# Low-rank products by sample on four column positions, with A copied for each sample

## The chip, the core and the metric
One NeuronCore of a Trainium2 chip runs the whole program. The metric is the device time of one execution in microseconds. The times are medians over runs; the profile is one further execution.

## The reference
```
x = x + einsum('bct,bcd->bdt', x, W0[cond])           # x 64x32x512, W0 16x32x32: mixes the 32 rows of a sample
base  = einsum('bsi,oi->bso', x, W)                   # W 512x512
low   = einsum('bsi,bir->bsr', x, lora_A[label])      # lora_A 5x512x32, label 0, 1 or 2 for each of 64 samples
delta = einsum('bsr,or->bso', low, lora_B_w) * 0.5    # lora_B_w 512x32
x = x + base + delta
```
Everything is float32. The kernel treats the label as any of 0 to 4.

## The kernel before
Four samples of 32 rows make a tile of 128 rows; there are 16 tiles, two to a pair, four to a quad. The two linear steps are taken in the other order: first u = x·(M) + delta for each tile, then the mix of the 32 rows of each sample with W0[cond] + identity. M is Wᵀ + identity, to which half the product of A0 (the A of label 0) and B is added in lora_half (L635). It is held as a rounded float32r part m_hi and the rest m_lo, x likewise as xt_hi and xt_lo, and main_tile (L579) makes 12 matmuls per tile from them: hi·hi, hi·lo and lo·hi for each of four chunks c of the 512 inputs.

For the other labels low_pair (L568) multiplies the differences A1..A4 minus A0, side by side in 128 columns (ad_hi, ad_lo), with the 256 rows of a pair, in 12 float32r matmuls. VectorE multiplies the result with keep, a mask by label and sample (keep_low, L450), ScalarE and VectorE split it into kept_hi and kept_lo, and fold_pair (L590) spreads the surviving block on TensorE. ScalarE copies it to low_stack (stack_low, L364), and delta_tile (L595) adds one matmul of low_stack with b_stack, which holds the rounded part and the rest of B/2 in turn.

Each engine has a queue of its own, written by hand, with semaphores between them. TensorE: six warm-up matmuls (L655), transposes of Bw, A, x rows and W with the ident matrix, the two halves of lora_half, then main_tile of the first pair in halves by columns. For each quad from the second on: low_pair, mix_quad (L604: 16 float32 products of 32x32 weights and 512 columns, on 4 row and 4 column positions), the main tiles with fold_pair between them, the delta tiles, low_pair for the second pair and its tiles. The last quad is mixed in three steps (mix_two, then mix_one twice) so that its output can be stored piece by piece. VectorE transposes x in blocks of 32 (transpose_x, L426), makes the lo parts (split_x, L438) and copies every second u out of PSUM (copy_u, L445); ScalarE makes the hi parts (L326), the other copies of u (L331) and the copies of y (L336). GpSimd makes the identity, the row numbers, a_diff (L290), ad_lo and 16 gathers of W0 rows (L264), and mix_of (L300) for each quad. SyncE issues B, the first x_rows, four parts of W, the second x_rows, A1..A4, then x pair by pair into two buffers, each load after the transposes that free its buffer, and the stores between them.

## Time and profile before

| | us |
|---|---|
| median of 3 runs | 84.39 (84.02 to 85.27) |
| profiled execution, its own time | 85.05 |
| its span, first to last instruction | 82.9 |
| TensorE matmuls busy | 76.3 (92%) |
| VectorE busy | 42.9 (52%) |
| ScalarE busy | 33.8 (41%) |
| GpSimd busy | 25.8 (31%) |
| mean granted TensorE clock | 0.986 |

PE is TensorE's matmul side and PEld its weight loads, which overlap; DVE is VectorE, ACT ScalarE, POOL GpSimd, SP SyncE; a q behind a name is that engine's sequencer. Times are us from the start of the span, L571 is line 571 of the kernel. A matmul's duration includes its way through the array, so the distance from one start to the next is what it costs in a row of matmuls. A group "x4" in a timeline is four instructions merged, with the time from the first start to the last end. The idle time stands in brackets with what ended it.

### The profile page before, as it was taken

Reading aid. Unit: us, or ns where it says so; the run is one execution under the profiler, and the core shown is the slowest. Engines: PE = TensorE matmul, PEld = TensorE weight load, DVE = VectorE, ACT = ScalarE, POOL = GpSimd, SP = SyncE. Lnnn points to the kernel's source line nnn. Section 1 sums busy time; section 2 is a strip of 40 time slices with the busy share of each in tenths; the row PEclk is TensorE's granted clock in tenths of the full one; section 3 lists DMA queues with packets and bytes.
Section 4 is the critical chain, followed back from the end, with each engine's and each line's share of the span. In section 5 each row is a group of like instructions: output and inputs, shape, how many; then the busy total and the mean of one; then the engine's idle time right before and its main releaser. Section 6 shows DMA issues by size and latency. Waiting matters only on the chain.

```text
span 82.9 us, 1563 instructions
## 1 busy us (share of the span) xinstructions
PE 76.3 (92%) x596; PEld 63.5 (77%) x596; DVE 42.9 (52%) x79; ACT 33.8 (41%) x70; POOL 25.8 (31%) x42
## 2 busy tenths in 40 slices
PE   4979999999999999999999999999999999999700
PEld 4489899999888588898885888988858887899300
DVE  3285666979932594059725950597269305202220
ACT  0625573624442286225422872254229622343320
POOL 4422786787878778750000200000003000000000
PEclk9999999999999999999999999999999999999995
DMA  0899999083280005797260049980000049705555
GB/s 9 274 270 362 172 202 159 17 209 76 70 199 16 13 11 133 207 249 223 73 180 0 0 124 219 205 214 6 0 4 0 0 95 211 201 8 111 142 127 126
DMA packets 13658, 10.18 MB, mean 123 GB/s; under 512 B 1748, under 2 KB 11348, under 8 KB 13652
## 3 DMA queue, kind: packets, MB, share of 16 engines
q1 hardware_dynamic: 12704, 9.64, 48.1%
q0 software_dynamic: 512, 0.26, 1.7%
q10 hardware_dynamic: 436, 0.20, 1.2%
q8 instruction: 4, 0.07, 0.3%
q14 instruction: 2, 0.02, 0.0%
HBM read 5.90 MB, written 4.19 MB: 122 GB/s over the span
## 4 chain that ended last, share of the span: by engine, by line
PE 83%; DMA 7%; SPq 4%; DVE 1%; issue 1%; DVEq 0%
PE p_u L586 16%; PE p_u L587 15%; PE p_u L588 15%; DMA x_rows<-in_x 7%; PE p_y L602 5%; PE p_low L572 5%; PE p_low L576 5%; PE p_low L571 5%; PE p_u L597 4%; SPq L209 3%; PE p_y L586 2%; PE p_y L587 2%; PE p_y L588 2%; PE p_fold L593 1%; PE p_fold L592 1%; PE p_fold L648 1%
## 5 line engine op out<-in xcount | busy, mean ns | idle before, releaser
L586 PE MATMUL p_u<-m_hi,xt_hi 128*128 128x512 f32 (+1 forms) x64 | 23.4, 365 | 0.0
L587 PE MATMUL p_u<-m_lo,xt_hi 128*128 128x512 f32 (+1 forms) x64 | 22.9, 358 | 0.0
L588 PE MATMUL p_u<-m_hi,xt_lo 128*128 128x512 f32 (+1 forms) x64 | 22.8, 356 | 0.0
L266 POOL DMA_INDIRECT w_sel<-in_L_cond_weights,w_row x16 | 16.2, 1011 | 4.6 <-issue 4.6
L428 DVE STREAM_TRANSPOSE xt<-x_sb 128x512 f32<-128x512 f32 x14 | 15.5, 1115 | 0.7 <-DMA x_sb<-in_x 0.7
L586 PEld LDWEIGHTS p_u<-m_hi,xt_hi 128*128 128x128 f32 x64 | 12.1, 189 | 4.3 <-issue 2.9
L448 DVE COPY u_sb<-p_u 128x512 f32<-128x512 f32 (+1 forms) x7 | 4.6, 654 | 18.0 <-PE p_u L597 18.0
L588 PEld LDWEIGHTS p_u<-m_hi,xt_lo 128*128 128x128 f32 x64 | 12.1, 189 | 1.9
L587 PEld LDWEIGHTS p_u<-m_lo,xt_hi 128*128 128x128 f32 x64 | 12.1, 189 | 1.3
L329 ACT ACTIVATE xt_hi<-xt 128x512 fp32r<-128x512 f32 x14 | 8.8, 630 | 4.8 <-DVE xt L428 4.7
L305 POOL TENSOR_TENSOR mix<-w_sel,fold_id 128x128 f32<-128x128 f32 x4 | 2.2, 550 | 25.4 <-PE p_y L602 25.3
L442 DVE TENSOR_TENSOR xt_lo<-xt,xt_hi 128x512 fp32r<-128x512 f32 x14 | 9.5, 683 | 0.8
L334 ACT ACTIVATE u_sb<-p_u 128x512 f32<-128x512 f32 x7 | 4.2, 599 | 10.8 <-PE p_u L597 10.8
L572 PE MATMUL p_low<-xt_lo,ad_hi 128*128 128x256 f32 x32 | 8.0, 283 | 0.0
L571 PE MATMUL p_low<-xt_hi,ad_hi 128*128 128x256 f32 x32 | 8.0, 282 | 0.0
L362 ACT ACTIVATE kept_hi<-kept 128x256 fp32r<-128x256 f32 x8 | 3.4, 419 | 10.7 <-DVE kept L454 10.7
L339 ACT ACTIVATE y_sb<-p_y 128x512 f32 (+1 forms) x12 | 6.8, 597 | 1.1 <-PE p_y L602 1.1
L572 PEld LDWEIGHTS p_low<-xt_lo,ad_hi 128*128 128x128 f32 x32 | 6.1, 191 | 0.2
L571 PEld LDWEIGHTS p_low<-xt_hi,ad_hi 128*128 128x128 f32 x32 | 6.1, 190 | 0.2
L454 DVE TENSOR_TENSOR kept<-p_low,keep 128x256 f32<-128x256 f32 x8 | 3.4, 424 | 5.0 <-PE p_low L576 4.9
L366 ACT ACTIVATE low_stack<-p_fold 128x256 fp32r<-128x256 f32 x8 | 3.0, 380 | 6.3 <-PE p_fold L593 6.3
L576 PE MATMUL p_low<-xt_hi,ad_lo 128*128 128x256 f32 x32 | 5.1, 282 | 0.0
(94 smaller groups left out, 95.7 us busy)
## 6 DMA issues: line engine op xcount, KB each, us to landing
x_sb<-in_x SPq DMA_DIRECT2D x28, 128.0 KB, 3.0
out<-y_sb SPq DMA_DIRECT2D x12, 256.0 KB, 4.0
w_sb<-in_L_cond_W SPq DMA_DIRECT2D x4, 256.0 KB, 4.3
x_rows<-in_x SPq DMA_DIRECT2D x2, 256.0 KB, 4.3
out<-y_two SPq DMA_DIRECT2D x4, 128.0 KB, 2.3
out<-y_one SPq DMA_DIRECT2D x6, 64.0 KB, 1.9
a_sb<-in_L_cond_lora_A SPq DMA_DIRECT2D x1, 256.0 KB, 6.6
w_sel<-in_L_cond_weights,w_row POOLq DMA_INDIRECT x16, 2.4
```

The lines of the kernel that those rows point to most:

```text
L266: nc.gpsimd.indirect_dma_start(out=w0_sel[:, t, :], out_offset=None, in_=W0_rows, in_offset=bass.IndirectOffsetOnAxis(ap=w0_row[:, t:t + 1 ...
L329: nc.scalar.activation(xt_hi[:, slot, :, P * u:P * (u + 1)], xt[:, u], COPY).then_inc(s_xhi, 1)
L339: nc.scalar.activation(y_sb[:, bass.ds(k, 1), i], p_y[i][:].unsqueeze(1), COPY).then_inc(s_y_copied, 1)
L428: nc.vector.transpose(xt[:, u].rearrange("p c (b s) -> p c b s", s=S), x_sb[:, slot, u].rearrange("p b (i c) -> p c b i", c=C)).then_inc(s ...
L442: nc.vector.tensor_tensor(xt_lo[:, slot, :, cols], xt[:, u], xt_hi[:, slot, :, cols].bitcast(F32), ALU.subtract).then_inc(s_xlo, 1)
L448: nc.vector.tensor_copy(u_sb[:, j, cols], bank[:, cols]).then_inc(s_u_odd, 1)
L571: mm(p_low[:, 0:ROWS], ad_hi[:, c], xt_hi[:, slot, c], start=(c == 0), stop=False)
L572: mm(p_low[:, 0:ROWS], ad_hi[:, c], xt_lo[:, slot, c], start=False, stop=False)
L576: last = mm(p_low[:, 0:ROWS], ad_lo[:, c], xt_hi[:, slot, c], start=False, stop=(c == C - 1))
L586: mm(to, xt_hi[:, slot, c, rows], m_hi[:, c, cols], start=(c == 0 and half != 1), stop=False)
L587: mm(to, xt_hi[:, slot, c, rows], m_lo[:, c, cols], start=False, stop=False)
L588: mm(to, xt_lo[:, slot, c, rows], m_hi[:, c, cols], start=False, stop=False)
```

## The change
- The low products are made sample by sample in float32. For a tile, a chunk c and a sample b, one matmul has the 32 columns of x of that sample as weights (128x32) and the 32 columns of that sample's A as moving data, and writes the 32 rows of the sample in p_low. The four samples of a tile lie on four column positions. 256 such calls take the place of 96 matmuls (low_group).
- Each sample's A comes from a_sel. For each quad GpSimd copies the first 8 samples' A (128x128 each) and ScalarE the other 8, with the offset read from the label into a register (select_a).
- VectorE copies the result four times side by side (copy_low), TensorE transposes it by tile (spread_low), ScalarE rounds all of it into low_stack, and VectorE puts the rest into the lower two of the four blocks (rest_of_low). b_stack holds B/2 rounded, rest, rounded, rest. The mask, the fold and both their splits go.
- Label 0 is no longer part of M: lora_half, the transposes of A and a_diff go. A is loaded whole, 320 KB in place of 64 + 256. B is loaded on ScalarE's queue, in rows of 512 bytes, no longer at the head of SyncE's; it is widened by ScalarE and transposed on TensorE after the first half main tile.
- low_group runs over tiles 0-1, 2-3 and then whole quads: the products of all four tiles of a quad are made at the start of that quad, ahead of its mix. xt holds four tiles of x instead of two. All loops over quads are written out.
- mix_two stands after the third main tile of the last quad, and the last delta product before mix_one.

```diff
-            sp.dma_start(bw_sb[:], Bw.rearrange("(o p) r -> p o r", p=P)).then_inc(s_bw_in, 16)
             sp.dma_start(x_rows[:, 0], x_tile[0]).then_inc(s_rows_in[0], 16)
             for o in W_ORDER:
                 sp.dma_start(w_sb[:, o], W[P * o:P * (o + 1), :]).then_inc(s_w_in[o], 16)
             sp.dma_start(x_rows[:, 1], x_tile[1]).then_inc(s_rows_in[1], 16)
-            sp.dma_start(a_sb[:, 1:NL].rearrange("p l c r -> p l (c r)"), A_cols[:, 1:NL]).then_inc(s_a_in, 16)
+            sp.dma_start(a_sb[:].rearrange("p (l n) -> p l n", l=NL), A_cols).then_inc(s_a_in, 16)
             load(1, 1)
...
-            pool.wait_ge(s_w0_row, BT)
-            for t in range(6):
-                gather(t)
+            def select_a(k):
+                first = QS * k
+                _, ats = nc.values_load_multi_w_load_instructions(
+                    a_at[0:1, first:first + HS], engines=(mybir.EngineType.Pool,), min_val=0,
+                    max_val=(NL - 1) * C * R,
+                    skip_runtime_bounds_check_because="the label was clamped to 0..NL-1 on the chip")
+                for i in range(HS):
+                    nc.gpsimd.tensor_copy(a_sel[:, first + i], a_sb[:, bass.ds(ats[i], C * R)]).then_inc(s_a_pool, 1)
...
+            pool.wait_ge(s_w0_row, BT)
+            pool.wait_ge(s_a_at, 2)
+            pool.wait_ge(s_a_in, 16)
+            select_a(0)
+            for t in range(4):
+                gather(t)
+            select_a(1)
             mix_of(0)
-            for t in range(6, TILES):
-                gather(t)
             for k in range(1, QUADS):
+                for t in range(4 * k, 4 * k + 4):
+                    gather(t)
+                if k < QUADS - 1:
+                    select_a(k + 1)
                 mix_of(k)
...
+                if k == 0:
+                    act.wait_ge(s_a_at, 2)
+                    act.wait_ge(s_a_in, 16)
...
+                for i in range(HS):
+                    nc.scalar.activation(a_sel[:, first + i], a_sb[:, bass.ds(ats[i], C * R)], COPY).then_inc(s_a_act, 1)
+            def stack_low(g):
+                cols = slice(P * (GROUPS[g][0] % 4), P * (GROUPS[g][-1] % 4 + 1))
+                act.wait_ge(s_fold, g + 1)
+                nc.scalar.activation(low_stack[:, cols], p_fold[:, cols], COPY).then_inc(s_stack, 1)
...
-            split_x(2, 1, 0)
-            split_x(3, 1, 1)
-            hi_kept(0)
+            keep_rows(0, p_low)
+            keep_rows(1, p_fold)
+            act.wait_ge(s_bT, 1)
+            nc.scalar.activation(b_stack[:].rearrange("q (p o) -> q p o", o=OC),
+                                 p_y[0][:].rearrange("q (o p) -> q p o", o=OC), COPY, scale=0.5).then_inc(s_bhi, 1)
+            split_x(2)
+            split_x(3)
+            select_a(0)
             stack_low(0)
-            hi_kept(1)
-            split_x(4, 0, 0)
-            split_x(5, 0, 1)
-            copy_u(0, 0, p_u[0])
+            copy_u(0, p_u[0])
+            select_a(1)
             stack_low(1)
-            copy_u(2, 2, p_y[2])
...
+                split_x(4 * k + 2)
+                split_x(4 * k + 3)
+                stack_low(k + 1)
                 copy_y(k - 1, 0)
-                split_x(2 * p + 2, 1, 0)
                 copy_y(k - 1, 1)
-                split_x(2 * p + 3, 1, 1)
-                stack_low(p)
+                copy_u(4 * k, p_u[0])
                 copy_y(k - 1, 2)
                 copy_y(k - 1, 3)
-                copy_u(2 * p, 0, p_u[0])
...
+                if k < QUADS - 1:
+                    split_x(4 * k + 4)
+                    split_x(4 * k + 5)
+                    select_a(k + 1)
+                copy_u(4 * k + 2, p_u[0])
...
+            def transpose_x(t):
+                p, u = t // 2, t % 2
+                slot = p % 2
+                if u == 0:
+                    dve.wait_ge(s_x_in[slot], 16 * Q * ((p + 1) // 2))
+                    if p >= 3:
+                        dve.wait_ge(s_xlo, 2 * p - 2)
+                        dve.wait_ge(s_low, (p - 2) // 2 + 2)
+                if p == 2:
+                    dve.wait_ge(s_low, 1)
+                nc.vector.transpose(xt[:, slot, u].rearrange("p c (b s) -> p c b s", s=S),
                                     x_sb[:, slot, u].rearrange("p b (i c) -> p c b i", c=C)).then_inc(s_xt, 1)
...
+            def copy_low(g):
+                n = len(GROUPS[g])
+                dve.wait_ge(s_low, g + 1)
+                nc.vector.tensor_copy(low_rep[:, 0:n], p_low[:, 0:R * n].rearrange("p (u r) -> p u r", u=n).unsqueeze(2)
+                                      .broadcast_to([P, n, Q, R])).then_inc(s_low_rep, 1)
+            def rest_of_low(g):
+                cols = slice(P * (GROUPS[g][0] % 4), P * (GROUPS[g][-1] % 4 + 1))
+                dve.wait_ge(s_stack, g + 1)
+                nc.vector.tensor_tensor(low_stack[2 * R:P, cols], p_fold[2 * R:P, cols],
+                                        low_stack[2 * R:P, cols].bitcast(F32), ALU.subtract).then_inc(s_stack_lo, 1)
...
+            transpose_x(2)
+            transpose_x(3)
+            split_x(2)
+            split_x(3)
+            copy_low(0)
+            dve.wait_ge(s_bhi, 1)
+            for j in (1, 3):
+                at = slice(R * j, R * (j + 1))
+                nc.vector.scalar_tensor_tensor(b_stack[at].rearrange("q (p o) -> q p o", o=OC),
+                                               p_y[0][at].rearrange("q (o p) -> q p o", o=OC), 0.5,
+                                               b_stack[at].bitcast(F32).rearrange("q (p o) -> q p o", o=OC),
+                                               ALU.mult, ALU.subtract).then_inc(s_blo, 1)
...
+            transpose_x(4)
+            rest_of_low(0)
+            transpose_x(5)
+            copy_u(1, p_u[1])
+            copy_low(1)
+            transpose_x(6)
+            rest_of_low(1)
+            transpose_x(7)
+            copy_u(3, p_y[3])
+            for k in range(1, QUADS):
+                t = 4 * k
+                more = k < QUADS - 1
+                copy_low(k + 1)
+                if k == 1:
+                    split_x(4)
+                    split_x(5)
+                if more:
+                    transpose_x(t + 4)
+                rest_of_low(k + 1)
+                split_x(t + 2)
+                split_x(t + 3)
+                if more:
+                    transpose_x(t + 5)
+                copy_u(t + 1, p_u[1])
+                if more:
+                    split_x(t + 4)
+                    split_x(t + 5)
+                    transpose_x(t + 6)
+                    transpose_x(t + 7)
+                    copy_u(t + 3, p_u[1])
+            copy_u(TILES - 1, p_u[1], left)
+            copy_u(TILES - 1, p_low, right, part=1)
             for i in range(2, BT):
...
+            def low_group(g):
+                for t in GROUPS[g]:
+                    at = t - GROUPS[g][0]
+                    quad, half = t // 4, t // 2 % 2
+                    if t % 2 == 0:
+                        if half == 0:
+                            pe.wait_ge(s_a_pool, HS * (quad + 1))
+                        else:
+                            pe.wait_ge(s_a_act, HS * (quad + 1))
+                    if t < 2:
+                        pe.wait_ge(s_rows_xt, t + 1)
+                    else:
+                        pe.wait_ge(s_xt, t - 1)
+                    for c in range(C):
+                        for b in range(BT):
+                            last = mm(p_low[S * b:S * (b + 1), R * at:R * (at + 1)],
+                                      xt[:, half, t % 2, c, S * b:S * (b + 1)],
+                                      a_sel[:, BT * t + b, R * c:R * (c + 1)], start=(c == 0), stop=(c == C - 1))
                 last.then_inc(s_low, 1)
-            def main_tile(bank, slot, u, cols=slice(0, O), half=None):
+            def spread_low(g):
+                pe.wait_ge(s_low_rep, g + 1)
+                for t in GROUPS[g]:
+                    last = mm(p_fold[:, P * (t % 4):P * (t % 4 + 1)], low_rep[:, t - GROUPS[g][0]], ident[:],
+                              start=(t == GROUPS[g][0]), stop=(t == GROUPS[g][-1]), is_transpose=True)
+                last.then_inc(s_fold, 1)
...
-            def fold_pair():
-                mm(p_fold[:, 0:ROWS], fold_to[:, 0], kept_hi[:], start=True, stop=False)
-                mm(p_fold[:, 0:ROWS], fold_to[:, 1], kept_lo[:], start=False, stop=True).then_inc(s_fold, 1)
...
-            pe.wait_ge(s_b_stack, 1)
-            pe.wait_ge(s_a_stack, 1)
-            lora_half(0)
...
             transpose_rows(1, p_fold)
-            lora_half(1)
             pe.wait_ge(s_xlo, 1)
             main_tile(p_u[0], 0, 0, left, half=0)
+            transpose_b(p_y[0])
             pe.wait_ge(s_xlo, 2)
             main_tile(p_u[1], 0, 1, left, half=0)
             main_tile(p_u[0], 0, 0, right, half=1)
-            pe.wait_ge(s_adhi, 1)
-            low_pair(0, waits=True)
             main_tile(p_u[1], 0, 1, right, half=1)
-            pe.wait_ge(s_xlo, 4)
-            pe.wait_ge(s_kept, 1)
-            low_pair(1)
-            pe.wait_ge(s_keptlo, 1)
-            fold_pair()
-            main_tile(p_y[2], 1, 0)
-            pe.wait_ge(s_stack, 1)
+            low_group(0)
+            pe.wait_ge(s_xlo, 3)
+            main_tile(p_y[2], 1, 0, chunks=(0, 1))
+            spread_low(0)
+            main_tile(p_y[2], 1, 0, chunks=(2, 3))
+            pe.wait_ge(s_bhi, 1)
+            pe.wait_ge(s_blo, 2)
+            pe.wait_ge(s_stack_lo, 1)
             delta_tile(p_u[0], 0)
...
-                main_tile(p_u[0], slot, 0)
-                pe.wait_ge(s_keptlo, p + 1)
-                fold_pair()
-                main_tile(p_u[1], slot, 1)
-                pe.wait_ge(s_stack, p + 1)
+            low_group(1)
+            pe.wait_ge(s_xlo, 4)
+            main_tile(p_y[3], 1, 1, chunks=(0, 1))
+            spread_low(1)
+            main_tile(p_y[3], 1, 1, chunks=(2, 3))
+            pe.wait_ge(s_stack_lo, 2)
+            delta_tile(p_y[2], 2)
+            delta_tile(p_y[3], 3)
+            def begin_quad(k):
+                low_group(k + 1)
+                pe.wait_ge(s_u_even, 2 * k)
+                pe.wait_ge(s_u_odd, 2 * k)
+                pe.wait_ge(s_mix, k)
+                if k > 1:
+                    pe.wait_ge(s_y_copied, BT * (k - 1))
+                mix_quad()
+                spread_low(k + 1)
+                pe.wait_ge(s_xlo, 4 * k + 1)
+                main_tile(p_u[0], 0, 0)
+                pe.wait_ge(s_stack_lo, k + 2)
                 delta_tile(p_u[0], 0)
+                pe.wait_ge(s_xlo, 4 * k + 2)
+                main_tile(p_u[1], 0, 1)
                 delta_tile(p_u[1], 1)
...
-            first_pair(1, None)
-            second_pair(1)
-            with pe.Fori(2, QUADS - 1) as k:
-                first_pair(k, BT * (k - 1))
-                second_pair(k)
-            first_pair(QUADS - 1, BT * (QUADS - 2))
-            pe.wait_ge(s_xlo, TILES)
-            low_pair(1)
-            copied(PAIRS - 1)
+                pe.wait_ge(s_u_even, 2 * k + 1)
+                pe.wait_ge(s_xlo, 4 * k + 3)
+                main_tile(p_u[0], 1, 0)
+                delta_tile(p_u[0], 2)
+                pe.wait_ge(s_u_odd, 2 * k + 1)
+                pe.wait_ge(s_xlo, 4 * k + 4)
+            for k in range(1, QUADS - 1):
+                begin_quad(k)
+                main_tile(p_u[1], 1, 1)
+                delta_tile(p_u[1], 3)
+            begin_quad(QUADS - 1)
             pe.wait_ge(s_mix, QUADS)
             pe.wait_ge(s_y_copied, BT * (QUADS - 1))
             mix_two()
-            main_tile(p_u[0], 1, 0)
-            pe.wait_ge(s_keptlo, PAIRS)
-            fold_pair()
             main_tile(p_u[1], 1, 1, left)
-            pe.wait_ge(s_stack, PAIRS)
-            delta_tile(p_u[0], 0)
-            delta_tile(p_u[1], 1, left)
+            delta_tile(p_u[1], 3, left)
             main_tile(p_low, 1, 1, right)
-            pe.wait_ge(s_u_even, PAIRS)
+            delta_tile(p_low, 3, right)
+            pe.wait_ge(s_u_even, TILES // 2)
             pe.wait_ge(s_two, BT)
             mix_one(p_y, 2)
-            delta_tile(p_low, 1, right)
-            pe.wait_ge(s_u_odd, PAIRS + 1)
+            pe.wait_ge(s_u_odd, TILES // 2 + 1)
             mix_one(p_end, 3)
```

## Rows read from the trace of the kernel before

**Rows 1.** The page: busy time by engine, and the chain that ended last by engine
```profile
PE 76.3 (92%) x596; PEld 63.5 (77%) x596; DVE 42.9 (52%) x79; ACT 33.8 (41%) x70; POOL 25.8 (31%) x42
...
PE 83%; DMA 7%; SPq 4%; DVE 1%; issue 1%; DVEq 0%
```
**Rows 2.** The chain in order of time, its start: start us, us, what
```profile
0.72 0.45 SPq L206
...
4.02 5.54 DMA x_rows<-in_x
...
9.70 0.72 PE p_fold L648 x4
10.43 0.48 PE p_y L638 x4
```
**Rows 3.** One quad as a stretch: us, busy us of each engine, clock, DMA
```profile
28.83:45.34 16.51, 16.51 (x123) 13.40 (x113) 9.48 (x15) 7.09 (x15) 6.06 (x7) 1.00 0.50 136
```
**Rows 4.** TensorE's timeline at the second quad's start: start, us, line, operands
```profile
26.24 0.28 PE L571 MATMUL p_low<-xt_hi,ad_hi 128*128 128x256 f32 x1
...
27.19 0.64 PE L576 MATMUL p_low<-xt_hi,ad_lo 128*128 128x256 f32 x4
27.76 1.14 PE L602 MATMUL p_y<-u_sb,mix 32*32 32x512 f32 x32
28.83 0.50 PE L586 MATMUL p_u<-m_hi,xt_hi 128*128 128x512 f32 x1
```
**Rows 5.** The chain in order of time, last quad
```profile
69.75 0.64 PE p_y L602 x32
...
73.16 0.23 PE p_u L588
73.39 0.12 PE p_fold L592
...
76.85 0.43 PE p_y L602 x32
```
**Rows 6.** TensorE's timeline, the last mix
```profile
78.11 0.34 PE L602 MATMUL p_u<-u_sb,mix 32*32 32x128 f32 x8 [0.52 <-DVE u_sb L448]
...
78.24 0.32 PE L602 MATMUL p_u<-u_sb,mix 32*32 32x128 f32 x8
```
**Rows 7.** TensorE's timeline, the start of the kernel
```profile
1.04 2.93 PE L655 MATMUL p_low<-warm 128*128 128x512 f32 x6 [1.04 <-DVE warm L465]
...
5.44 0.64 PE L659 MATMUL p_u<-ident,a_rep 128*128 128x128 f32 x4
5.92 0.65 PE L648 MATMUL p_low<-ident,x_rows 128*128 128x128 f32 x4
```
**Rows 8.** Groups by line and shape: busy us, mean ns, idle before
```profile
L266 POOL DMA_INDIRECT w_sel<-in_L_cond_weights,w_row x16 | 16.2, 1011 | 4.6 <-issue 4.6
L428 DVE STREAM_TRANSPOSE xt<-x_sb 128x512 f32<-128x512 f32 x14 | 15.5, 1115 | 0.7 <-DMA x_sb<-in_x 0.7
...
L262 POOL TENSOR_TENSOR w_sb<-w_sb,ident 128x128 f32<-128x128 f32 x2 | 0.9, 458 | 3.2 <-DMA w_sb<-in_L_cond_W 3.2
...
L414 ACT ACTIVATE y_one<-p_y 128x128 f32<-128x128 f32 x4 | 0.8, 282 | 1.5 <-PE p_y L602 1.5
...
L244 POOL MEMSET ident<- 128x128 f32 x1 | 0.2, 205 | 0.1
```
**Rows 9.** ScalarE's timeline: two issues, and the second pair's last split_x
```profile
1.19 0.64 ACTq L317 DMA_DIRECT2D ids_i<-in_itok_B  x1
1.86 0.24 ACTq L318 DMA_DIRECT2D ids_i<-in_itok_B  x1
...
15.88 0.63 ACT L329 ACTIVATE xt_hi<-xt 128x512 fp32r<-128x512 f32 x1 [0.38 <-DVE xt L428]
```
**Rows 10.** GpSimd's timeline where A has landed
```profile
11.27 1.30 POOL L290 TENSOR_TENSOR a_diff<-a_sb 128x512 f32<-128x512 f32 x1 [0.30 <-DMA a_sb<-in_L_cond_lora_A]
```

359 lines of the change are left out of this document (112 added, 247 removed).

## The prediction
> **What bounds the kernel now.** I read the page first: the matmul side of TensorE is busy for 92% of the span and makes up 83% of the chain that ended last; the only other large piece of that chain is one transfer [rows 1]. So the end moves by what is added to or taken from TensorE's own queue, plus whatever makes that queue wait. The chain in order of time says where it begins: the loads on SyncE's queue, the second x_rows landing at 9.57 us, four transposes of it at 9.70, then the last products of A0 and B, and from 10.7 on matmuls without a gap [rows 2]. Between two quad starts, 28.83 to 45.34, TensorE is busy for the whole 16.51 us while VectorE has 9.48 and ScalarE 7.09 [rows 3]: both have room, so work put on them is free only if it is ready in time.
>
> **What one quad contains now.** The timeline of a quad's start shows the units. The 12 products of low_pair run from 26.24 to 27.67 (8 at 0.12 us apart, then 4 more from 27.19): 1.44 us per pair. Mixing takes until 28.83: 1.07 us for 16 calls of 512 columns [rows 4]. The chain further on has the fold at 0.12 us for each of two products, and the mixes with 256 and 128 columns at 0.64 and 0.43 us [rows 5].
>
> **Taken off TensorE's queue.** low_pair: 8 x 1.44 = 11.5 us. fold_pair: 8 x 0.24 = 1.9. The second half of lora_half stands on the chain with 0.48 [rows 2] and goes. The transposes of Bw and A and the first half of lora_half lie in the start, where the transfers set the time, so they give nothing. B's load leaves the head of SyncE's queue, where it takes one issue of 0.45 us before x_rows and w [rows 2]; everything behind it is issued 0.5 us sooner, and 64 KB less lies ahead of it. I take 0.5 us. Sum: 14.4 us.
>
> **Put on TensorE's queue.** (a) The products by sample. Per tile there are 16 calls (4 chunks by 4 samples) of 128 rows, 32 columns of weights and 32 columns moving, four of them on four column positions. The nearest row is the mix, also float32 and also 32 columns wide, though on 32 rows. Its three sizes fit a line: 0.43 us for 256 more columns is 1.67 ns a column, and 0.21 us is left over for no columns [rows 5, 4]. Since 1.67 ns is four clocks at 2.4 GHz while 16 calls run at once, the positions do work side by side. Each call is two matmul records (32 records for 16 calls); at the same position the second set starts 0.13 us after the first, at 78.24 against 78.11, with 128 columns in each [rows 6]: 0.107 of streaming and 0.026 on top. With 32 columns a record is then 0.027 + 0.026 = 0.053 us, a position gets 8 of them per tile, and four positions side by side give 0.43 us per tile, 6.9 for 16. Bounds: 0.21 per tile if the 0.026 hides (3.4 in all), and 32 x 0.053 = 1.7 us per tile if the positions take turns (27 in all). I take 0.43, since the mix is the nearest row. (b) Going into and out of the narrow form: the mix leaves 0.21, and 0.09 pass before it (27.67 to 27.76), so 0.3 each for the two groups that stand between full products, and half of it for the three that lie beside a mix: 1.05 us. (c) spread_low: 16 transposes at the pace of the present ones, 0.48 us for four [rows 7] : 1.9 us, as much as the folds. (d) transpose_b is now on the path: 0.48 us, as much as lora_half gave. (e) The last delta product moves ahead of the last mix but one: 0.12 us. Sum: 10.45 us. Without waits the change is worth 14.4 - 10.45 = 3.95 us.
>
> **New waits.** The copies of A by sample are the new work beside TensorE: 8 on GpSimd and 8 on ScalarE for each quad, each after 8 labels were loaded into registers. A ScalarE copy of 128x128 took 282 ns with 0.8 us for four, so about 0.2 each [rows 8]. A register load has no row: the bounds I take from the nearest sequencer rows, the issue of a transfer, 0.24 once for all eight or 0.64 for each, 0.2 to 5.1 us [rows 9], and I take 1.5, nearer the lower end, because eight values are asked for together. That makes select_a about 3.1 us on ScalarE (1.8 to 6.7). The Trainium skill (DMA: Bandwidth & Descriptors, Latency and other measured facts) gives a load of a tensor into registers a floor of about 600 ns; with that as the whole cost, an estimate of 2.2 us for select_a would leave about 0.4 us of the waits below. No row here shows it.
> Where it falls: the last split_x of the second pair starts at 15.88 on ScalarE now [rows 9] and will end near 16.2. select_a(0) runs to 19.3, stack_low(0) to 19.7. TensorE starts its main products at 9.7 in place of 10.74, and with transpose_b, low_group(0) and the third main tile it wants low_stack at 20.1. VectorE has to be there too, with two passes over b_stack that read PSUM with a stride and a transpose of 1115 ns [rows 8] ahead of rest_of_low(0): 20.4 to 21. I put the first wait at 0.8 us. Then copy_u(0), select_a(1), stack_low(1), rest_of_low(1) take 1.9 + 3.1 us from the delta on, and TensorE has 4.7 us of its own work: 0.4 us. Each further us of select_a costs two here. Sum of waits: 1.2 us.
> Behind that I find cover. From the second quad on, select_a(k+1) on ScalarE stands behind four copy_y and two split_x and ends some 1.5 us before low_group asks for it. GpSimd begins select_a(0) when A has landed, about when a_diff starts now, 11.27 [rows 10]; eight copies between the 0.205 of a memset and the 0.458 of a two-input add [rows 8], say 0.4 with their gap, and the load end near 15.5, with 0.5 us left before low_group(0). Four gathers of 1.0 us each plus 0.3 of issue and a second select_a end near 25, with 1 us left before low_group(2). If that cover is gone, each us there costs one. The mask and the two splits of kept leave VectorE and ScalarE, which only adds slack. SyncE's queue is otherwise as before; load_next now follows transposes that wait for a whole quad's products, but each has several us until its tile is needed.
>
> **Sum.** 14.4 - 10.45 - 1.2 = 2.75 us less. The profiled execution took 85.05 us with a span of 82.9; it would take 82.3. The median of the runs is 84.39, 0.66 below it, so I forecast 81.7 us.
>
> **Rivals.** *The positions take turns* (slower). Here all four share the 128 rows, whereas the mix has separate rows too. If products at different positions only streamed one after the other, a tile would cost 32 x 0.027 = 0.86 us, 6.9 us more than forecast: 88.6; with the 0.026 as well it is 27 us for all, 102. It decides from 0.6 us per tile on, where the gain is gone. Against it: in the last mix eight records of one bank, on the same 32 rows and four column positions, last 0.34 us together, where each streams 0.107 [rows 6]. The Trainium skill (TensorE: Matmul & The Clock Gate, The mechanism) speaks for it: a weight load overlaps products in flight only when its row group differs. By that rule the time would be the 88.6 to 102 of this rival.
> *The copies come late.* If registers cost 0.5 us each, select_a is 5.6 us on ScalarE, 2.5 more than taken, which costs 2 x 2.5 = 5 us: 86.7. For it: no row prices the loads; and ScalarE's select_a stands ahead of stack_low in its queue. Against it: one load for eight values.
> *The clock falls.* In the start TensorE now does transposes of Bw, A, x and W and two sets of ordinary products; afterwards only transposes with gaps and one small product. Today the six first products took 2.93 us, 0.49 each, against 0.23 for the same size later [rows 5]: the lower of the two levels, 1.2 GHz, at first, and the full one by 5.44 [rows 7]. If the clock is at the lower level when the main products begin and needs as long as at the start, 4.4 us, to rise, half of that is lost: 81.7 + 2.2 = 83.9.
>
> **Chances.** Forecast as worked out 50% (79.3 to 82.9), clock 15% (83.9), late copies 17% (83.5 to 87), turns 13% (87 to 102), better than forecast, because the 0.026 hides, 5% (78). A measurement of this kernel tells about 2%, 1.7 us, from no change, so faster is below 82.7: 0.52; within 82.7 to 86.1: 0.25; slower: 0.23. The range 79.3 to 86.8 leaves out the turns and the best case.
>
> **What would show it.** Right: a low_group of four tiles takes 1.7 to 2.0 us between its first matmul and the mix; the quad from one mix's end to the next takes 15.4 us instead of 16.5; main products begin near 9.7; TensorE's gaps before the delta products near 20 and 25 us sum to 1.2. Wrong: low_group at 3 us or more (turns); ScalarE still copying A when TensorE waits for stack_low (late copies); main products at 0.24 us for 256 columns (clock); or TensorE waiting for GpSimd's copies before low_group(0) or (2), which I hold to be covered by a small margin only.

## The result and the profile after

The changed kernel takes 79.56 us (median of 4 runs, 79.33 to 80.97) against 84.83 us of the kernel before on the same chip (4 runs, 84.02 to 86.47): 0.940 of it, with a 95% interval of 0.928 to 0.952. Here and below medians are over all runs of a kernel, and ratios and their intervals over its fast runs, those within 1.5% of its fastest. The forecast of 81.7 us had the sign right, and the time lies inside the range, 0.3 us above its low end of 79.3; but the gain is about twice what the sum gave. Profiled execution against profiled execution it went from 85.05 to 79.59 us, 5.46 less where 2.75 were expected.

The page after, its busy line and the chain by engine:
```profile
PE 70.6 (91%) x1000; PEld 55.4 (71%) x1000; DVE 42.6 (55%) x67; ACT 36.7 (47%) x92; POOL 32.7 (42%) x73
...
PE 86%; DVE 4%; ACT 1%; issue 1%
```
TensorE is still the bound, with 5.7 us less of its own work than in [rows 1]. The transfer that made up 7% of the chain is gone from it, and VectorE's share has risen from 1% to 4%.

The start after, TensorE's timeline (start, us, line, operands; answers to [rows 7] and [rows 2]):
```profile
1.06 2.93 PE L667 MATMUL p_low<-warm 128*128 128x512 f32 x6 [1.06 <-DVE warm L492]
3.79 1.05 PE L653 MATMUL p_low<-ident,x_rows 128*128 128x128 f32 x4
...
5.12 3.31 PE L643 MATMUL p_y<-ident,w_sb 128*128 128x128 f32 x16
8.26 0.65 PE L653 MATMUL p_fold<-ident,x_rows 128*128 128x128 f32 x4
8.67 0.36 PE L602 MATMUL p_u<-m_hi,xt_hi 128*128 128x256 f32 x1
```
The transposes of x begin right behind the warm-up, nothing stands between W's transposes and the second x rows, and the main products begin at 8.67 us instead of 10.74. Only the first line has idle time in brackets. In before the first piece behind the warm-up had some too:
```profile
4.56 1.08 PE L659 MATMUL p_u<-ident,bw_rep 128*128 128x128 f32 x4 [0.60 <-DVE bw_rep L479]
```
The 8.67 is one execution's figure: in the eleven traces of the changed kernel and its variants that do this work at the start the main products begin between 8.34 and 10.11 us, and in the two of before at 10.74 and 11.96.

The first delta products after, same view, and then the chain that leads to them:
```profile
17.50 0.47 PE L602 MATMUL p_y<-m_hi,xt_hi 128*128 128x512 f32 x1
...
19.63 0.70 PE L608 MATMUL p_u<-b_stack,low_stack 128*128 128x512 f32 x2 [0.49 <-DVE low_stack L475]
```
```profile
16.48 0.68 DVE b_stack L521
17.19 0.70 DVE b_stack L521
17.92 1.11 DVE xt L441
19.06 0.44 DVE low_stack L475
```
This is the one wait for another engine that the change brought. The same six products take 1.48 us at the second place (22.59 to 24.07) and 2.13 here, so it costs 0.65.

A quad in the middle, as a stretch (us, then busy us of PE, PEld, DVE, ACT, POOL, clock, DMA; answers to [rows 3]), and TensorE's timeline of the group at its end (answers to [rows 4]):
```profile
42.86:57.71 14.85, 14.85 (x226) 11.64 (x217) 9.31 (x12) 7.66 (x19) 4.64 (x5) 1.00 0.37 96
```
```profile
55.27 1.40 PE L582 MATMUL p_low<-a_sel,xt 128*32 128x32 f32 x128
56.63 1.15 PE L613 MATMUL p_y<-u_sb,mix 32*32 32x512 f32 x32
57.71 0.66 PE L591 MATMUL p_fold<-ident,low_rep 128*128 128x128 f32 x4
```
Four tiles of low products go from 55.27 to 56.63, 1.36 us for 128 records, 0.34 us a tile. The quad takes 14.85 us in place of 16.5. The full quad ahead of it takes 15.64 (27.22 to 42.86), of which 0.68 is a pause in its mix that is shown below; in after_ref, a later profile of the same kernel, both take 14.8 to 14.9. What this says of the forecast is worked out behind the experiments.

### The profile page after: what moved, and what is told of

Its sections match the earlier page's. It is cut to its first block, busy times and chain, and to the rows that moved or that the text cites. A ratio compares the mean times of both kernels' runs of the same rounds, so it can differ in the third digit from the quotient of the medians.

```text
span 77.8 us, 2452 instructions
## 1 busy us (share of the span) xinstructions
PE 70.6 (91%) x1000; PEld 55.4 (71%) x1000; DVE 42.6 (55%) x67; ACT 36.7 (47%) x92; POOL 32.7 (42%) x73
## 4 chain that ended last, share of the span: by engine, by line
PE 86%; DVE 4%; ACT 1%; issue 1%
PE p_u L602 16%; PE p_u L603 16%; PE p_u L604 16%; PE p_low L582 7%; PE p_y L613 7%; PE p_u L608 4%; PE p_y L643 4%; PE p_low L667 4%; PE p_fold L591 3%; DVE b_stack L521 2%; PE p_y L602 1%; DVE xt L441 1%; PE p_y L604 1%; PE p_y L603 1%; PE p_low L653 1%
## 5 line engine op out<-in xcount | busy, mean ns | idle before, releaser
L265 POOL DMA_INDIRECT w_sel<-in_L_cond_weights,w_row x16 | 16.5, 1029 | 4.4 <-issue 4.4
L331 ACT ACTIVATE xt_hi<-xt 128x512 fp32r<-128x512 f32 x14 | 8.1, 624 | 8.6 <-PE p_u L608 6.7
L278 POOL COPY a_sel<-a_sb 128x128 f32 x32 | 9.7, 346 | 2.2 <-issue 2.2
L336 ACT ACTIVATE u_sb<-p_u 128x512 f32<-128x512 f32 x7 | 4.2, 595 | 10.8 <-PE p_u L608 10.6
L365 ACT ACTIVATE a_sel<-a_sb 128x128 f32 x32 | 6.8, 296 | 1.4 <-issue 1.4
L582 PEld LDWEIGHTS p_low<-a_sel,xt 128*32 128x32 f32 x512 | 5.3, 110 | 1.7 <-issue 1.4
L341 ACT ACTIVATE y_sb<-p_y 128x512 f32<-128x512 f32 x12 | 6.5, 599 | 0.0
L582 PE MATMUL p_low<-a_sel,xt 128*32 128x32 f32 x512 | 6.0, 199 | 0.0
L608 PE MATMUL p_u<-b_stack,low_stack 128*128 128x512 f32 (+1 forms) x14 | 5.3, 387 | 0.5 <-DVE low_stack L475 0.5
L371 ACT ACTIVATE low_stack<-p_fold 128x512 fp32r<-128x512 f32 (+1 forms) x5 | 2.6, 514 | 6.0 <-PE p_fold L591 6.0
L613 PE MATMUL p_y<-u_sb,mix 32*32 32x512 f32 (+2 forms) x160 | 5.3, 492 | 0.0
L468 DVE COPY low_rep<-p_low 128x512 f32<-128x512 f32 (+1 forms) x5 | 2.9, 585 | 2.4 <-PE p_low L582 2.3
```

Of the source, the lines that this page charges most:

```text
L265: nc.gpsimd.indirect_dma_start(out=w0_sel[:, t, :], out_offset=None, in_=W0_rows, in_offset=bass.IndirectOffsetOnAxis(ap=w0_row[:, t:t + 1 ...
L278: nc.gpsimd.tensor_copy(a_sel[:, first + i], a_sb[:, bass.ds(ats[i], C * R)]).then_inc(s_a_pool, 1)
L331: nc.scalar.activation(xt_hi[:, slot, :, P * u:P * (u + 1)], xt[:, slot, u], COPY).then_inc(s_xhi, 1)
L365: nc.scalar.activation(a_sel[:, first + i], a_sb[:, bass.ds(ats[i], C * R)], COPY).then_inc(s_a_act, 1)
L582: last = mm(p_low[S * b:S * (b + 1), R * at:R * (at + 1)], xt[:, half, t % 2, c, S * b:S * (b + 1)], a_sel[:, BT * t + b, R * c:R * (c + 1 ...
L608: mm(bank[:, cols], low_stack[:, P * u:P * (u + 1)], b_stack[:, cols], start=False, stop=True).then_inc(s_u, 1)
```

## The experiments

Twelve runs were made on three chips. On the first one the kernel before took 95.44 us (median of 13 runs, 93.42 to 99.02), on the second 85.08, on the third 84.76, so times are compared within one chip only. In the kernels that leave out or replace part of the low products (e_no_copies, e_wide, e_narrow) the result is not the reference's.

**Ten microseconds slower: the first chip.** Its four runs were meant for the wait, the copies and the place of B's load.

after_again is the changed kernel itself.

> The changed kernel once more, beside the other three. Both theories of the 0.65 us hole in the third mix (41.15 to 41.82 in its trace, while the other mixes of 512 columns take 1.07 us) are told apart: if the kernel makes it, it stands at the same call again; if that one execution made it, it is gone and the profiled time is 0.6 us lower. Time near 79.5 us.

e_b_early makes B's stack earlier, on ScalarE ahead of keep_rows and on VectorE ahead of the third and fourth block of x:
```diff
-            keep_rows(0, p_low)
-            keep_rows(1, p_fold)
             act.wait_ge(s_bT, 1)
             ...
+            keep_rows(0, p_low)
+            keep_rows(1, p_fold)
...
-            transpose_x(2)
-            transpose_x(3)
-            split_x(2)
-            split_x(3)
-            copy_low(0)
             dve.wait_ge(s_bhi, 1)
             ...
+            transpose_x(2)
+            transpose_x(3)
+            split_x(2)
+            split_x(3)
+            copy_low(0)
```


> ScalarE rounds b_stack ahead of its two copies of x, and VectorE makes b_stack's rests ahead of transpose_x(2), in the 0.9 us in which it waits for a load. Nothing is left out. Theory (the wait before the first delta product is VectorE's queue: two b_stack passes of 0.7 and a transpose of 1.1 ahead of rest_of_low): TensorE's wait of 0.8 us between the third main tile and the delta goes, and the time falls by 0.5 to 0.8 against the changed kernel. Rival (ScalarE's copies of A hold stack_low back, as I forecast in part): rest_of_low(0) still comes late and the time stays.

e_no_copies drops both select_a, with TensorE's waits for them, and reads a_sb's label 0 in low_group:
```diff
-                                      a_sel[:, BT * t + b, R * c:R * (c + 1)], start=(c == 0), stop=(c == C - 1))
+                                      a_sb[:, R * c:R * (c + 1)], start=(c == 0), stop=(c == C - 1))
```


> Leaves out select_a on both engines, copies and register loads; every sample uses the A of label 0, read in place. Theory (the trace shows 1.7 us for eight copies on ScalarE and 1.9 on GpSimd with the loads hidden, and TensorE never waiting for them): the time stays within 0.4 us of the changed kernel. Rival (the forecast: copies cost 1.2 us of waits): it falls by 1 us or more.

e_b_head puts B's load back at the head of SyncE's queue:
```diff
+            sp.dma_start(bw_sb[:].rearrange("p o r -> p (o r)"), Bw_cols).then_inc(s_bw_in, 16)
             sp.dma_start(x_rows[:, 0], x_tile[0]).then_inc(s_rows_in[0], 16)
...
-            act.dma_start(bw_sb[:].rearrange("p o r -> p (o r)"), Bw_cols).then_inc(s_bw_in, 16)
```


> B's load goes back to the head of the sync queue, in its new layout; nothing is left out. Theory of the forecast (the head of the queue delays x_rows and W by one issue and 64 KB): main products begin 0.4 to 0.6 us later than 8.67 and the time rises by as much. Rival (in the start TensorE itself is the bound, since it makes transposes without a gap on the lower clock up to 6.6 us): less than 0.2 us.

Measured: after_again 86.26 us (83.39 to 88.1), e_b_early 84.91 (0.906 of before, 0.900 to 0.913), e_no_copies 83.73 (0.884, 0.871 to 0.897), e_b_head 85.1 (0.907, 0.901 to 0.912). The gain over before is larger here than on the chip of the result, yet the four are 4 to 7 us slower than the changed kernel was there. The kernel before is slower on this chip too, by 10.6 us, with granted clocks of 0.93 to 0.96 in its runs. TensorE's timeline of after_again at the first group of low products shows where:
```profile
16.47 0.58 PE L582 MATMUL p_low<-a_sel,xt 128*32 128x32 f32 x43
17.28 0.26 PE L582 MATMUL p_low<-a_sel,xt 128*32 128x32 f32 x4 [0.24 <-issue]
18.00 0.27 PE L582 MATMUL p_low<-a_sel,xt 128*32 128x32 f32 x3 [0.46 <-issue]
18.76 0.27 PE L582 MATMUL p_low<-a_sel,xt 128*32 128x32 f32 x5 [0.49 <-issue]
19.52 0.33 PE L582 MATMUL p_low<-a_sel,xt 128*32 128x32 f32 x9 [0.48 <-issue]
19.78 0.50 PE L602 MATMUL p_y<-m_hi,xt_hi 128*128 128x512 f32 x1
...
20.84 0.63 PE L602 MATMUL p_y<-m_hi,xt_hi 128*128 128x512 f32 x1
```
"issue" means that the instruction waited for no semaphore that the profile shows. The group took 3.3 us instead of 0.84, the second one 2.6 instead of 0.69, with steps of 0.7 us, while the later groups took 1.3 to 1.4 as before. After these pauses the granted clock fell to the lower level, 1.2 GHz, from 20.25 to 23.67 us, and the products there are 0.43 us apart instead of 0.23. The other three show the same steps in the same two groups, e_no_copies too, so the copies don't make them. The four times therefore say little about the edits. In e_b_early the wait before the first delta products is absent, but it is absent in after_again too, behind the pauses. One reading stands: in e_b_head the main products began at 9.00 us, as in e_b_early and before after_again's 10.11, so B's place in SyncE's queue is worth less than executions differ.

**Does this happen to the kernel before?** before_again is that kernel, profiled on the second chip.

> The kernel before, unchanged, for its trace on the same chip as the others of this call. On the last chip the kernels with the change had three to five pauses of about 0.7 us each on TensorE inside their first two groups of low products. If the pauses belong to the low products by sample, before has none of its own of over 0.5 us between 11 and 30 us, and its span stays at 82 to 84 us. If they belong to the chip or to the count of instructions that TensorE has issued, before has pauses of the same length too, at 250 to 290 and 410 to 440 recorded instructions.

It took 86.31 us in its one run, with a span of 84.1, and no pause of over 0.5 us between 11 and 30 us other than the usual 0.52 behind the mix. But the three variants of the changed kernel that ran on the same chip had no pauses of 0.7 us in their first two groups either; the longest is one of 0.27 us in the second group of e_narrow, which takes 1.05 us instead of 0.67. So the run doesn't tell apart what it was meant to; the long pauses in those two groups have been seen on one chip only, and there is no trace of before from it. That before itself loses 10.6 us on that chip speaks against the low products as their only ground. One row of its start matters below:
```profile
5.33 1.09 PE L659 MATMUL p_u<-ident,bw_rep 128*128 128x128 f32 x4 [1.37 <-DVE bw_rep L479]
```

**What a low product costs.** e_in_turn only swaps the two loops, so that the four products of a position in a tile, eight records, follow each other:
```diff
-                    for c in range(C):
-                        for b in range(BT):
+                    for b in range(BT):
+                        for c in range(C):
```


> Same products, same count, another order: the eight products of one position follow each other, then those of the next position. If positions overlap only where neighbouring products are at different positions, a tile costs 32 records of 0.0317 = 1.01 us instead of the 0.33 to 0.34 of the changed kernel: 0.68 us more each, 10.8 us over sixteen tiles, about 90 us where the changed kernel takes 79.6. If the queue of products overlaps them whatever their order, the time is the same within 0.5 us. Overlap only where one position ends and the next begins would give 29/32 of the first.

e_wide and e_narrow change the number of moving columns (and e_wide, in a line not shown, the columns of p_low that it writes):
```diff
-                                      a_sel[:, BT * t + b, R * c:R * (c + 1)], ...
+                                      a_sel[:, BT * t + b, R * (c % 3):R * (c % 3 + 2)], ...     (e_wide, 64)
+                                      a_sel[:, BT * t + b, R * c:R * c + R // 2], ...            (e_narrow, 16)
```


> Each low product moves 64 columns of A instead of 32 (its result is not the reference's: the second half is a product with the neighbouring block). If the 0.0317 us between two products of a position are their columns passing through, it becomes about 0.058 to 0.063, and a group of four tiles takes 4 x 8 x 0.060 = 1.9 to 2.1 us or more instead of 1.35, 2.3 to 3 us on the whole. If it is a fixed price of an instruction, the group stays at 1.35 and the time too, within 0.4 us.

> Each low product moves 16 columns of A instead of 32 (half of every low product is left out). If columns set the spacing, the products of a position follow each other after about 0.02 us and a group of four tiles takes 1.0 us or less instead of 1.35: 1.4 us less on the whole. If a product has a fixed price (the issue of 32 instructions at four positions, or their loads), group and time stay within 0.4 us.

Medians: e_in_turn 84.49 us (0.982 of before, 0.975 to 0.989), e_wide 81.84 (0.959, 0.954 to 0.965), e_narrow 79.96 (0.941, 0.937 to 0.946). The changed kernel did not run on this chip, so e_narrow stands in for it; its ratio to before is that of the changed kernel elsewhere (0.940 and 0.941). TensorE's timelines at the last group, one kernel each:
```profile
58.77 2.74 PE L582 MATMUL p_low<-a_sel,xt 128*32 128x32 f32 x128
61.44 1.14 PE L613 MATMUL p_y<-u_sb,mix 32*32 32x512 f32 x32
```
```profile
57.70 1.99 PE L582 MATMUL p_low<-a_sel,xt 128*32 128x64 f32 x128
59.62 1.16 PE L613 MATMUL p_y<-u_sb,mix 32*32 32x512 f32 x32
```
```profile
55.40 1.32 PE L582 MATMUL p_low<-a_sel,xt 128*32 128x16 f32 x128
56.71 1.15 PE L613 MATMUL p_y<-u_sb,mix 32*32 32x512 f32 x32
```
From the group's start to the mix that is 2.67 us in turn, 1.92 with 64 columns and 1.31 with 16, against 1.36 with 32 in the changed kernel. In the single records the starts of the four positions lie 7 ns apart and a position's next record follows after 0.056 us (64 columns), 0.032 (32) and 0.032 (16). So the columns set the pace at 64, and at 32 a fixed price has taken over: both theories of the two expectations hold, each on its side. The columns alone account for 0.053 of the 0.056, by the 0.83 ns a column that the forecast had from [rows 6]; the fixed price is 0.032 us for each record of a position, or 0.008 us for each record of the group. It belongs to the position: in e_in_turn, where one position is alone at first, its records also start 0.032 us apart. Only the second record of a position comes later, 0.052 us behind the first with 16 or 32 columns and 0.080 with 64. The 32 records that a position has in a group of four tiles are 1.02 us at this pace; most of the other 0.3 of the group's 1.32 to 1.36 are this first distance, 0.05 to 0.08 between its two halves, and 0.16 from the last record to the mix.

In turn, a tile costs 0.67 us, 0.021 a record: twice the changed kernel's, but not the 1.01 of the first theory. A position starts 0.153 us behind the one before it, while that one is still at work, so two of them overlap in this order, and all four if neighbours are at different positions. Over 16 tiles the groups take 10.9 us instead of 5.7, and the time is 0.982 of before instead of 0.941: about two thirds of the gain hang on the order of two loops.

**The wait, the copies and the start, on the third chip.** The measure is after_ref, the changed kernel.

> The changed kernel once more, as the measure for the others of this call: 79.3 to 81 us, span 77.5 to 79. The wait before the first delta products (0.49 us shown, 0.77 us with what it costs beside it) should be there again. The pause of 0.65 us inside the third mix stays at the same call if it belongs to the program and is gone or elsewhere if it belongs to one execution.

> The same order as e_b_early: the two pieces of B's stack and the low rows of B are made ahead of the third and fourth block of x, on VectorE and ScalarE. If the wait before the first delta products comes from VectorE still making B's stack (0.68 and 0.70 us) ahead of the low rows, it goes: 0.5 to 0.8 us faster than after_ref. If something else is late right behind it (x's third block, 1.11 us on VectorE), the wait moves to the next main products and the time stays within 0.3 us.

> Leaves out every copy of A by sample (GpSimd and ScalarE) and the register loads for them; each sample uses the A of label 0. If the copies are hidden as the profile shows (TensorE waited for none), the time is within 0.4 us of after_ref. If they hold ScalarE back where it evicts u and mix, or contend with the other engines, it is 1 to 2 us faster.

e_start_work adds the work that the change took out of the start (extra() is four products of 128x256 into p_u[0], which the main products overwrite):
```diff
+            for c in range(C):
+                mm(p_u[1][:, P * c:P * (c + 1)], ident[:], ident[:], start=(c == 0), stop=(c == C - 1),
+                   is_transpose=True)
             transpose_w(0)
             transpose_w(1)
+            extra()
             ...
             transpose_rows(1, p_fold)
+            extra()
```


> The changed kernel with work of the size that the change took out of the start put back on TensorE, with no other use: four 128x128 float32 transposes ahead of W's, four 128x256 products after the second quarter of W, four after the second rows of x. In before these were A's transposes (0.48 us) and the products of A and B for M (0.55 and 0.56). If TensorE's own work sets the start, the main products begin 1.3 to 1.9 us later than in after_ref and the whole is as much slower. If the landing of W and of x sets it, only the last four count: 0.5 to 0.7 us.

Medians: after_ref 79.22 us (78.4 to 79.69; 0.941 of before, 0.934 to 0.948), e_b_early2 79.93 (79.0 to 81.34; 0.940, 0.930 to 0.951), e_no_copies2 79.62 (79.31 to 81.76; 0.944, 0.936 to 0.952), e_start_work 80.51 (79.97 to 81.79; 0.953, 0.944 to 0.961).

*The copies* are hidden from TensorE: from the first main product to the first single-tile mix TensorE takes 61.53 us without them against 61.58. The time is the same within 0.4 us too, but not for that reason alone: without the copies the profiled span is 0.2 us shorter, with the main products 0.5 later and the stores at the end 0.6 quicker, and 3.0 us lie outside the span instead of 1.8. After's timelines of ScalarE and of GpSimd say why:
```profile
15.46 1.71 ACT L365 ACTIVATE a_sel<-a_sb 128x128 f32 x8 [0.29 <-issue]
17.79 0.39 ACT L371 ACTIVATE low_stack<-p_fold 128x256 fp32r<-128x256 f32 x1 [0.61 <-PE p_fold L591]
...
36.28 1.71 ACT L365 ACTIVATE a_sel<-a_sb 128x128 f32 x8 [1.07 <-issue]
...
11.20 1.94 POOL L278 COPY a_sel<-a_sb 128x128 f32 x8 [2.17 <-issue]
...
18.39 1.94 POOL L278 COPY a_sel<-a_sb 128x128 f32 x8
```
ScalarE is ready 0.61 us before the transposed low rows are, and GpSimd 1.9 us before the first group. The register loads are not free where nothing runs beside them: ahead of its third set ScalarE idles for 1.07 us, and GpSimd's first copy starts 1.07 to 1.08 us after A has landed in all ten traces with copies (10.12 to 11.20 in after).

*The start* is TensorE's own work to a large part. TensorE's timeline of e_start_work:
```profile
5.12 1.11 PE L681 MATMUL p_u<-ident 128*128 128x128 f32 x4
6.02 1.57 PE L643 MATMUL p_y<-ident,w_sb 128*128 128x128 f32 x8
7.35 0.72 PE L668 MATMUL p_u<-warm 128*128 128x256 f32 x4
7.91 1.14 PE L643 MATMUL p_y<-ident,w_sb 128*128 128x128 f32 x8
8.89 0.65 PE L653 MATMUL p_fold<-ident,x_rows 128*128 128x128 f32 x4
9.29 0.72 PE L668 MATMUL p_u<-warm 128*128 128x256 f32 x4
```
The added pieces (L681, L668) take 0.91, 0.55 and 0.55 us, 2.01 in all, and the main products begin at 9.85 instead of 8.34: 1.51 later, inside the 1.3 to 1.9 of the first theory. Against the other two traces of this chip, with 8.81 and 8.85, it is 1.0. The median is 1.3 us higher, the ratio by 0.012, about 1.0 us, with intervals that just overlap. In none of these four traces does TensorE wait between the warm-up and the main products. That is not so everywhere: in six of the twelve traces it waits there for a part of W or for x's rows, 0.2 to 1.4 us in all, as in e_narrow's timeline:
```profile
8.57 0.75 PE L643 MATMUL p_y<-ident,w_sb 128*128 128x128 f32 x4 [0.66 <-POOL w_sb L261]
```
So the transfers are not far behind TensorE, and a start with still less of its own work would probably gain less, which was not tried.

*The wait* goes as expected. TensorE's timeline of e_b_early2:
```profile
17.48 0.48 PE L602 MATMUL p_y<-m_hi,xt_hi 128*128 128x512 f32 x1
...
18.95 0.63 PE L608 MATMUL p_u<-b_stack,low_stack 128*128 128x512 f32 x2
```
The six products take 1.47 us, against 2.11 in after_ref, and nothing is late right behind them. Still the kernel isn't faster: 0.940 of before against 0.941, where 0.5 to 0.8 us less was expected. In the profiled execution pauses take the gain back; whether they do in its other executions is not recorded. Here is the group and mix in TensorE's timeline, first of e_b_early2, then of the changed kernel as first profiled:
```profile
39.34 1.37 PE L582 MATMUL p_low<-a_sel,xt 128*32 128x32 f32 x128
40.67 2.15 PE L613 MATMUL p_y<-u_sb,mix 32*32 32x512 f32 x32
...
```
```profile
39.78 1.36 PE L582 MATMUL p_low<-a_sel,xt 128*32 128x32 f32 x128
41.10 1.83 PE L613 MATMUL p_y<-u_sb,mix 32*32 32x512 f32 x32
42.86 0.33 PE L591 MATMUL p_fold<-ident,low_rep 128*128 128x128 f32 x1
```
This mix takes 2.08 and 1.76 us where 1.08 is the rule (after_ref's own, and all others here); e_no_copies2 loses 0.35 at the same place. e_b_early2 also has 1.82 us in the third group instead of 1.3, and on the first chip e_no_copies loses 0.6 at this mix. So the pause is not in every execution, but it comes most often at this call; e_start_work's (0.74 us step, 0.4 more than the rule) came at 58.24, in the first main tile behind a mix. No edit of mine beats the changed kernel.

## Why the forecast was right in sign and half the size

That the time fell inside the range is in part luck. None of the four things that the forecast named as signs of being right came as stated: a group of four tiles took 1.36 us and not 1.7 to 2.0, a quad 14.85 and not 15.4, the main products began at 8.67 and not near 9.7, and TensorE's gaps before the delta products are 0.5 (0.65 with their cost) and not 1.2. Each missed to the same side, and the 5% given to "better than forecast" was for one of them alone.

By stretches of TensorE's queue, before against after, with the forecast's own terms sorted into them:

| stretch | before | after | forecast | measured |
|---|---|---|---|---|
| start to the first main product | 10.74 | 8.67 | -0.98 | -2.07 |
| first main product to first mix | 17.02 | 17.48 | +1.55 | +0.46 |
| first mix to third mix over full quads | 33.02 | 30.48 | -2.02 | -2.54 |
| from there to the first single-tile mix | 16.00 | 14.48 | -1.32 | -1.52 |
| from there to the end of the span | 6.08 | 6.68 | 0 | +0.60 |
| outside the span | 2.19 | 1.80 | 0 | -0.39 |

The measured column adds up to -5.46, the forecast's to -2.77 (its 2.75 but for rounding). The third row holds the pause of 0.68; in after_ref the same stretch takes 29.67.

**The start: "so they give nothing".** This step was wrong in its mechanism, by 1.1 us in the profiled pair. The size is less sure than that, since the start differs by up to 1.8 us between executions of kernels with the same start. The chain of [rows 2] led through the landing of the second x_rows at 9.57 us, and I took all of TensorE's work ahead of it as free. But before's TensorE had a chain of its own nearly as long, and waited for that landing only 0.18 us: it waited for B's widened rows before anything else (0.60 us in the profiled execution, 1.37 in before_again, rows above), then did the transposes of B and of A and the first half of lora_half. The change removed both at once, the work and the late landing. e_start_work shows the part that is TensorE's: putting back 2.01 us costs 1.0 to 1.5. The 0.5 us I gave to B's load I can't confirm as an effect on the queue; what its load held up was TensorE's first transposes.

**The low products: "0.027 + 0.026".** The mechanism was right, four positions side by side on the same 128 rows; the size was off. The second term was read off the only distance that a mix with two records per position has, from the first to the second (0.133 us with 128 columns), and taken for every record. The runs show it as a price of the first distance alone: 0.080 against 0.056 later with 64 columns, 0.052 against 0.032 with 32. Later records take the larger of their columns (0.053 us at 64) and about 0.032. That makes 0.26 us a tile, and 0.34 with the ends of a group, where 0.43 was taken without them; 5.7 us for all groups of after, with its slower first and third one, where 6.9 were expected. At 1.2 us this is the largest miss of a single term. **Positions take turns** is refuted for this order, and priced for the other by e_in_turn: 0.67 us a tile, lower than the 0.86 of the rival. The Trainium skill (TensorE: Matmul & The Clock Gate, The mechanism) lets a weight load overlap running products only where the row group differs; here every load and every product has all 128 rows, and four of them start within 0.02 us of each other. The measurement decides.

**Into and out of the narrow form.** The 1.05 us came, but all of it ahead of the first mix: there the 48 half-width and 24 full products around the new pieces take 11.96 us instead of 11.24, the first behind each piece 0.32 instead of 0.23, and the delta pairs 0.27 us more. In a full quad it is nothing: delta products +0.1, main products -0.1. spread_low came to 0.41 us for four and 0.14 for two, 1.5 in all, 0.4 under the folds' pace.

**The waits.** One of two came. The first cost 0.65 where 0.8 was said, and it was VectorE's, which the forecast had last too: two passes over b_stack (0.68 and 0.70) and a transpose of x (1.11) stand ahead of the low rows; ScalarE was early. The second, 0.4, didn't come. Its term was select_a at 3.1 us on ScalarE: the first took 2.0, since the load of eight registers shows as 0.29 us and not 1.5. Where nothing covers it the load costs 1.07 us, not far from the 1.5; what the forecast missed is that most of it runs beside the instruction ahead. The Trainium skill (DMA: Bandwidth & Descriptors, Latency and other measured facts) has a floor of about 600 ns for such a load; the trace shows 0.29 us of idle time ahead of ScalarE's first copies, and 1.07 for eight values where the load is exposed. With that, **the copies come late** falls, and TensorE's 61.53 us in e_no_copies2 confirm it.

**The clock** had risen by 6.59 us (5.51 in before), well ahead of the main products. In the twelve traces of the changed kernel and its variants the rise lies between 3.9 and 10.7 us, and before_again has it at 8.47, so the change isn't what moves it. Only in e_wide did it come behind the first main product, and cost the first twelve 1.88 us instead of 1.51.

**The end.** TensorE gained there what the sum said and 0.2 more, and 0.6 went back at the stores, which no step had looked at; SyncE's issues set the end there, starting 1.50 us behind the first single-tile mix in both kernels. SyncE's queue at the stores of the last two tiles, first before, then after_ref, then e_in_turn:
```profile
78.28 1.78 SPq L229 DMA_DIRECT2D out<-y_one  x4
80.17 0.87 SPq L234 DMA_DIRECT2D out<-y_one  x2
```
```profile
71.42 2.43 SPq L224 DMA_DIRECT2D out<-y_one  x4
73.96 0.85 SPq L229 DMA_DIRECT2D out<-y_one  x2
```
```profile
77.42 1.77 SPq L224 DMA_DIRECT2D out<-y_one  x4
```
The four issues take 0.66 us longer in after_ref, and the two behind them are that much later. It isn't the new order of the last delta product, which e_in_turn has as well. What goes with it is one line of the page on the DMA queues, first after, then e_in_turn:
```profile
q8 instruction: 8, 0.13, 0.7%
```
```profile
q8 instruction: 7, 0.11, 0.6%
```
The eighth transfer of instructions begins at 72.02 us in after_ref, amid the four issues. In all eight traces in which one begins beside them (at most 0.2 us ahead of the first issue, or amid them: after, after_ref, after_again, e_b_early, e_b_early2, e_b_head, e_narrow, e_start_work), the four issues take 2.40 to 2.55 us; in the six that have none (both of before, e_in_turn, e_wide, both without copies) they take 1.77 or 1.78. No run adds or removes that transfer alone.

**What stays open.** First, 0.39 us outside the span: 2.2 us in both traces of before, 1.8 in all with the change but the two without copies, which have 3.0 and 3.2. In the untraced runs before has 1.8 to 3.1, so part of the 0.39 is one execution's. Second, the pauses. Before has 4 transfers of instructions, after 8, and TensorE has 1,000 recorded matmuls instead of 596, at the densest 128 with as many loads in 1.3 us. The pauses fall into low groups or right behind them in most cases, and e_in_turn and e_wide, whose groups are slower, had none of over 0.15 us. That fits a queue that at times isn't refilled fast enough. The Trainium skill (Runtime: NRT & Kernel Launch, Instruction fetch mechanics) says that such refills are mostly hidden; at the stores the trace speaks against it. For the pauses of TensorE no row ties one to a refill (the transfer ahead of the pause at 41.17 had ended at 40.50), and after_ref and e_narrow, as dense as after, lose only 0.4 each, so it is argued and not shown. It wasn't tried to make the same products with other work between two refills.

## What to carry to other kernels

When a chain ends in a transfer, look how long the engine's own queue is up to the same point, and how long it really waited for the transfer (0.18 us here): a change that shortens both can gain where the chain shows nothing. Look at a start in several traces before a gain there is put down to anything. Don't add a fixed price found at one size to a streaming price at another, and don't read a pace from the first two records; find out which price is hidden, by a size on either side. And where a change doubles the number of instructions, count their transfers in the page and look what runs beside the last of them.

## What of the hardware was unexpected

- Float32 products of 128 rows and 32 columns of weights at four column positions run side by side: starts 7 ns apart, one position's next after 0.032 us, the same for 16 and 32 moving columns, 0.056 for 64. Only the second record of a position comes about 0.02 us later than this.
- The order of calls is worth a factor of two: 0.34 us a tile with the position changing at each call, 0.67 with it changing every fourth call.
- A load of eight register values costs 1.07 to 1.08 us on GpSimd behind a landing (ten traces) and shows as 0.95 to 1.07 us of idle time ahead of ScalarE's third set in nine of ten. Ahead of ScalarE's first two sets it shows as 0.29 us and less than 0.1.
- TensorE can stall without a semaphore, in single steps of up to 0.7 us: by 0.15 us or less a group in e_in_turn and e_wide, 0.4 to 1.7 us in all in the other six traces of the changed kernel and its variants off the first chip, and 1.3 to 3.3 us in each of the first two groups on it.
- Issuing four stores takes 0.66 us longer where a transfer of instructions begins beside it: 2.40 to 2.55 us in eight traces, 1.77 or 1.78 in the six without.
